# Layer-3 products of a four-layer conditional residual network as fp32 products on halves of the TensorE array

## What is computed

```python
x = x + L0(x)   # x @ W0.T + b0 + scale * (x @ A0[id0].T) @ B0[id0]   rank 16, 8 adapters
x = x + L1(x)   # x @ W1.T + b1 + (x @ A1[id1].T) @ B1[id1].T         rank 16, 32 adapters
x = x + einsum('bsi,boi->bso', x, W2[id2])     # one of 8 matrices 1024 x 1024 for each batch
x = x + einsum('bct,bcd->bdt', x, W3[id3])     # one of 16 matrices 64 x 64, over the 64 tokens
```

## Time and profile before

| | us |
|---|---|
| median of 3 runs | 582.42 (582.11 to 583.15) |
| the profiled execution | 582.33 |
| its span (first to last instruction) | 580.5 |
| PE busy | 571.4 (98% of the span) |
| DVE busy | 326.8 (56%) |
| ACT busy | 282.0 (49%) |
| line 1302, the transposes: 256 matmuls | 35.9 |

### The profile page before, as it was taken

How to read it: one execution, slowest core, us unless ns; L and a number is a source line. 1 busy time by engine, 2 the same in 40 slices (tenths; PEclk the granted TensorE clock), 3 DMA queues, 4 the chain that set the end, 5 groups by cost and what they waited for, 6 DMA issues and landing times.

```text
span 580.5 us, 10596 instructions
## 1 busy us (share of the span) xinstructions
PE 571.4 (98%) x2710; PEld 478.6 (82%) x2711; DVE 326.8 (56%) x583; ACT 282.0 (49%) x370; POOL 56.0 (10%) x87
## 2 busy tenths in 40 slices
PE   8999999999999999999999999999999989999997
PEld 7888888888878888888888888888888878888885
DVE  6985211122777557944455795545588568745320
ACT  5632210214645738646273865536386648455211
POOL 3240000200000300001030000004000202000000
PEclk9999999999999999999999999999999999999999
DMA  8755835101207223453221445322233632230103
GB/s 305 266 176 66 87 99 199 40 20 54 91 25 268 74 56 131 149 183 93 57 63 48 136 124 213 88 60 60 52 126 100 246 87 78 61 101 5 37 2 73
DMA packets 66014, 60.92 MB, mean 105 GB/s; under 512 B 42050, under 2 KB 50242, under 8 KB 65988
## 3 DMA queue, kind: packets, MB, share of 16 engines
q1 hardware_dynamic: 65988, 60.63, 35.4%
HBM read 49.33 MB, written 11.27 MB: 104 GB/s over the span
## 4 chain that ended last, share of the span: by engine, by line
PE 96%; DVE 2%; DMA 1%; ACT 0%; issue 0%; DVEq 0%; POOL 0%; SPq 0%; POOLq 0%
PE y_ps L1271 29%; PE y_ps L1313 27%; PE y_ps L1221 11%; PE t_ps L1221 6%; PE t_ps L1302 5%; PE low_ps L1261 3%; PE y_ps L1341 3%; PE y_ps L1202 2%; PE y_ps L1198 1%; PE low_ps L1202 1%; PE t_ps L1202 1%; PE y_ps L1287 1%; PE y_ps L1286 1%; PE y_ps L1327 1%; PE t_ps L1212 1%; DMA arena<-w 1%
## 5 line engine op out<-in xcount | busy, mean ns | idle before, releaser
L1271 PE MATMUL y_ps<-wm,ops 128*128 128x512 f32 x768 | 179.7, 391 | 0.0
L1271 PEld LDWEIGHTS y_ps<-wm,ops 128*128 128x128 f32 x768 | 141.9, 188 | 29.0 <-DVE arena L1001 0.2
L1313 PE MATMUL y_ps<-ring,ops 128*128 128x512 f32 x696 | 165.3, 390 | 0.0
L1313 PEld LDWEIGHTS y_ps<-ring,ops 128*128 128x128 f32 x696 | 128.9, 188 | 25.5
L581 ACT CAST ops<-arena 128x512 fp32r<-128x512 f32 x32 | 19.7, 620 | 90.6 <-PE y_ps L1271 90.6
L1221 PE MATMUL y_ps<-ring,wm 128*128 128x512 f32 x240 | 55.3, 390 | 0.0
L1221 PEld LDWEIGHTS y_ps<-ring,wm 128*128 128x128 f32 x240 | 44.9, 188 | 9.3
L994 DVE TENSOR_TENSOR ring<-arena,ring 128x1024 fp32r<-128x1024 f32 x40 | 47.7, 1227 | 2.5 <-ACT ring L612 1.7
L483 POOL TENSOR_TENSOR arena<-arena,ident 128x128 f32<-128x128 f32 x40 | 28.3, 727 | 179.4 <-DMA arena<-wt 176.8
L612 ACT CAST ring<-arena 128x1024 fp32r<-128x1024 f32 x40 | 40.5, 1050 | 5.5 <-POOL arena L483 2.3
L1008 DVE TENSOR_TENSOR arena<-arena,ops 128x512 f32<-128x512 f32 x32 | 22.3, 696 | 36.0 <-ACT arena L635 26.3
(11 more groups left out here) (153 smaller groups left out, 635.9 us busy)
## 6 DMA issues: line engine op xcount, KB each, us to landing
arena<-wt SPq DMA_DIRECT2D x48, 512.0 KB, 4.4
arena<-xt SPq DMA_DIRECT2D x32, 256.0 KB, 2.8
out<-arena SPq DMA_DIRECT2D x30, 256.0 KB, 3.1
arena<-w SPq DMA_DIRECT2D x8, 576.0 KB, 5.3
a_stage<-a_tab SPq DMA_DIRECT2D x64, 64.0 KB, 1.9
arena<-b_tab SPq DMA_DIRECT2D x64, 64.0 KB, 2.0
arena<-a_cols SPq DMA_DIRECT2D x8, 256.0 KB, 4.2
a_tab<-bias SPq DMA_DIRECT2D x4, 256.0 KB, 8.4
```

Source lines behind the costliest of these rows:

```text
L1271: op = nc.tensor.matmul(y_ps[:, cols], xs[:, k, part_x, :], wm[:, k, part_w, cols], start=k == 0 and part_x == part_w, stop=False)
L1313: op = nc.tensor.matmul(y[:, cols], xs2[:, k, part_x, :], ring[:, k, part_w, cols], start=k == 0 and part_x == part_w, stop=k == KT - 1 an ...
```

## The change

The transposes become fp32 products without any splitting. For each block of 128 features and each batch there is one product: stationary operand the batch's 64 token rows by 128 features of x2 (rows 0 to 63 or 64 to 127 of the array), moving operand that batch's 64 x 64 matrix. The 16 results of a pair are 64 columns each, the first batch's in one bank of t_ps and the second's in the other, so both banks hold the whole pair, and one block stands where there were two. The splits of x2 and of the matrix go, `xs2_hi` becomes one copy and `xs2_lo` one subtraction for each half, and the second half's copy waits for the first half's subtraction.

Four things come with it. Pair 0's `main_part` and `lora_b` write y2_ps (`main_ps`) and wait for one more product of M. In pair 1 the first half of `main_part` stands ahead of `low_products`, the transposes of pair 0 stand between, and `between_loras` comes two feature blocks later; VectorE's steps 0 and 1 are reordered. SyncE loads the second half of slot 0 (with b0's columns) first, then A1's columns, then the first half; ScalarE and TensorE use the halves as they come. `WARM_UPS` is 9 in place of 11. `layer3_of(j)` waits for `t_done` and is issued a pair later.

```diff
-WARM_UPS = 11
+WARM_UPS = 9
...
+        def main_ps(j):
+            return y2_ps if isinstance(j, int) and j == 0 else y_ps
...
-            load_slot(0)
+            half = HK * P
+            sp.dma_start(slot(0)[:, half:FEATS + N0_COLS], w0[0][:, half:]).then_inc(w0_part_in, 16)
+            sp.dma_start(slot(0)[:, FEATS + N0_COLS:], a1_cols[0]).then_inc(a1_in[0], 16)
+            sp.dma_start(slot(0)[:, 0:half], w0[0][:, 0:half]).then_inc(slot_in[0], 16)
...
             def layer3_of(j):
-                sp.wait_ge(w3_lo_ready, j)
+                sp.wait_ge(t_done, j)
                 load_w3(j)
...
+                if k == 0:
+                    act.wait_ge(w0_part_in, 16)
+                    nc.scalar.copy(w0_blocks(k, 0, second), w0_of[:, second]).then_inc(w0_part_hi, 1)
                 act.wait_ge(a1_in[k % STAGES], 16 * (k // STAGES + 1))
                 nc.scalar.copy(a1[:, k, 0, :], slot(k)[:, FEATS + N0_COLS:]).then_inc(a1_hi, 1)
                 act.wait_ge(w0_folded, k + 1)
-                nc.scalar.copy(w0_blocks(k, 0), ...).then_inc(w0_hi, 1)
+                if k == 0:
+                    nc.scalar.copy(w0_blocks(k, 0, first), w0_of[:, first]).then_inc(w0_hi, 1)
...
             def xs2_hi(j, h, second):
                 def parts(by_batch):
-                    act.wait_ge(t_done, 2 * j + (h + 1))
+                    act.wait_ge(t_done, j + 1)
+                    if h == 1:
+                        act.wait_ge(xs2_lo_ready, 2 * j + 1)
                     if not (isinstance(j, int) and j == 0):
                         act.wait_ge((half_used, l2_done)[h], j)
-                    nc.scalar.copy(xs2_of(h, 0, by_batch), t_of(0)).then_inc(xs2_hi_ready, 1)
-                    nc.scalar.copy(t_lo_of(h), t_of(1)).then_inc(t_lo_ready, 1)
+                    nc.scalar.copy(xs2_of(h, 0, by_batch), t_of(h)).then_inc(xs2_hi_ready, 1)
...
                 dve.wait_ge(y_done, j + 1)
                 if not (isinstance(j, int) and j == 0):
-                    dve.wait_ge(xs2_lo_ready, 2 * j)
-                nc.vector.tensor_tensor(x2, y_ps[:, :], bias[:, :], ALU.add).then_inc(x2_ready, 1)
+                    dve.wait_ge(t_done, j)
+                nc.vector.tensor_tensor(x2, main_ps(j)[:, :], bias[:, :], ALU.add).then_inc(x2_ready, 1)
...
+                    dve.wait_ge(xs2_hi_ready, 2 * j + (h + 1))
+                    nc.vector.tensor_tensor(xs2_of(h, 1, by_batch), t_of(h), xs2_of(h, 0, by_batch),
+                                            ALU.subtract).then_inc(xs2_lo_ready, 1)
...
-                    pe.wait_ge(w0_hi, k + 1)
-                    for i in range(KT):
+                    if k == 0:
+                        pe.wait_ge(w0_part_hi, 1)
+                        pe.wait_ge(a1_hi, 1)
+                    else:
+                        pe.wait_ge(w0_hi, k + 1)
+                    for i in (*SECOND_HALF, *FIRST_HALF):
+                        if k == 0 and i == 0:
+                            pe.wait_ge(w0_hi, 1)
...
-                for k in range(HK):
-                    cols = slice((h * HK + k) * P, (h * HK + k + 1) * P)
-                    to = t_ps[:, 2 * k * P:2 * (k + 1) * P]
-                    for part_x in range(2):
-                        op = nc.tensor.matmul(to, x2_split[:, part_x, cols], w3_split[:, :, :].rearrange("p s r -> p (s r)"),
-                                              start=part_x == 0, stop=part_x == 1)
+                pe.wait_ge(x2_ready, j + 1)
+                pe.wait_ge(w3_folded, j + 1)
+                if not (isinstance(j, int) and j == 0):
+                    pe.wait_ge(xs2_lo_ready, 2 * j)
+                for k in range(KT):
+                    for b in range(2):
+                        r, to = slice(b * ROWS, (b + 1) * ROWS), b * BANK + k * ROWS
+                        op = nc.tensor.matmul(t_ps[:, to:to + ROWS], x2[r, k * P:(k + 1) * P], w3_stage[r, r],
+                                              start=True, stop=True)
...
+            def first_step():
+                low_products(0)
+                pe.wait_ge(m_lo, KT - 1)
+                main_part(0, 0)
+                between_loras(0)
+                pe.wait_ge(m_lo, KT)
+                main_part(0, 1)
+                lora_b(0)
+
+            def second_step():
+                pe.wait_ge(x_lo_ready, 3)
+                main_part(1, 0)
+                low_products(1)
+                transposes(0)
+                main_part(1, 1, {KT - 2: lambda: between_loras(1)})
+                lora_b(1)
+                layer2(0, lambda: transposes(1))
```

More of the change, by code:

```diff
@@ L529, in a_split_of, with w0_blocks @@
             return a_split[:, :, cols].rearrange("p k (b r) -> p b k r", b=2)
-        def w0_blocks(k, part):
-            return wm[:, :, part, k * P:(k + 1) * P]
+        def w0_blocks(k, part, blocks=slice(0, KT)):
+            return wm[:, blocks, part, k * P:(k + 1) * P]
         @block.scalar
@@ L536, in _ @@
             for k in range(KT):
+                w0_of = slot(k)[:, 0:FEATS].rearrange("p (i m) -> p i m", m=P)
+                first, second = slice(0, HK), slice(HK, KT)
+                if k == 0:
+                    act.wait_ge(w0_part_in, 16)
+                    nc.scalar.copy(w0_blocks(k, 0, second), w0_of[:, second]).then_inc(w0_part_hi, 1)
                 act.wait_ge(a1_in[k % STAGES], 16 * (k // STAGES + 1))
@@ L1263, in low_products, with main_part @@
                 op.then_inc(low_done, 1)
-            def main_part(h, between=None):
+            def main_part(j, h, between={}):
                 for k in (FIRST_HALF, SECOND_HALF)[h]:
-                    if between and k == KT - 1:
-                        between()
+                    if k in between:
+                        between[k]()
                     for part_x, part_w in SPLIT:
                         for cols in BANKS:
-                            op = nc.tensor.matmul(y_ps[:, cols], xs[:, k, part_x, :], wm[:, k, part_w, cols],
+                            op = nc.tensor.matmul(main_ps(j)[:, cols], xs[:, k, part_x, :], wm[:, k, part_w, cols],
                                                   start=k == 0 and part_x == part_w, stop=False)
@@ L1361, in layer2 @@
                     batch_half(y_ps, 0, 1, tiles=True)
-                    between(0)
+                    between()
                     pe.wait_ge(xs2_lo_ready, 2 * i + 2)
@@ L1373, in layer2 @@
                         batch_half(y2_ps, 1, 0)
-                        between(1)
                 with pe.Else():
@@ L1388, in layer2, with step @@
                     else:
-                        layer2_half(y, 1, between=lambda: between(1))
-            def step(j, before=1):
-                low_products(j)
-                if not (isinstance(j, int) and j == 0):
-                    pe.wait_ge(x2_ready, j)
-                else:
-                    pe.wait_ge(m_lo, KT - 2)
-                if before >= 2:
-                    pe.wait_ge(first_taken, j - 1)
-                main_part(0)
-                between_loras(j)
-                if before == 0:
-                    pe.wait_ge(m_lo, KT)
-                if before == 1:
-                    transposes(0, 0)
-                main_part(1, (lambda: transposes(0, 1)) if before == 1 else None)
+                        layer2_half(y, 1)
+            def first_step():
[14 more added lines that the diff above has]
+                layer2(0, lambda: transposes(1))
+            def step(j):
+                low_products(j)
+                pe.wait_ge(x2_ready, j)
+                pe.wait_ge(first_taken, j - 1)
+                main_part(j, 0)
+                between_loras(j)
+                main_part(j, 1)
                 lora_b(j)
-                if before >= 1:
-                    layer2(j - 1, lambda h: transposes(j, h))
+                layer2(j - 1, lambda: transposes(j))
             pe.wait_ge(ident_ready, 1)
@@ L1428, in _ @@
             pe.wait_ge(plan_ready, 1)
-            step(0, before=0)
-            step(1)
+            first_step()
+            second_step()
             with pe.Fori(2, PAIRS) as j:
-                step(j, before=2)
-            layer2(PAIRS - 1, lambda h: None, y=y_ps, last=True)
+                step(j)
+            layer2(PAIRS - 1, lambda: None, y=y_ps, last=True)
 def kernel(x, itok_B_1_7, itok_B_6_15, itok_B_3_7, itok_B_0_15, L0_cond_weight, L0_cond_bias,
```

90 lines of the change are left out of this document (23 added, 67 removed).

## The result

| | before | after |
|---|---|---|
| median | 582.41 us (8 runs, 581.95 to 585.28) | 585.18 us (8 runs, 584.25 to 587.69) |
| ratio | | 1.005, 95% interval 1.0032 to 1.0068 |
| profiled execution, span | 582.33, 580.5 | 587.69, 585.7 |
| mean granted clock in the profiled execution | 0.999 | 0.996 |

Slower by 0.5%, which is 2.8 us: a small loss, but clear of zero, where no change was forecast.

What follows compares the result with a forecast made beforehand. The prediction took TensorE to bound the kernel, busy for all 25.75 us of a pair. 582.33 + 2.9 - 2.1 - 1.15 gave 582.0 us, no change, with a range of 574 to 592.

Steps and rivals of the forecast that it cites:

- Terms 1 and 2: Transposes of 16 pairs: old blocks out, 30.7 us; new fp32 products in, 33.6 us; together +2.9 us.
- Rival 1: New transpose blocks: loads of the two halves queue, 3.86 us a block, +31.0 us, 610.1 us; chance 0.16.
- rival 2: New transpose blocks: no price for going in and out, 1.81 us a block, 577.3 us; chance 0.16.
- Rival 3: Start: fewer warm-ups make the clock rise later, start term +0.7 us, 583.8 us; chance 0.04 within the main case.
- its list of what would show it: Signs in the trace: block about 2.1 us, pair about 25.9, no PE wait over 0.3 between 169 and 187, low-part products at 7.8.
- Term 3: Pair 1, up to layer 2: about 2.1 us of TensorE waits all go, -2.1 us.
- The check on what is late next: Pair 1: finish_low(1) would end about 183.4 and TensorE want it at 183.8, fitting by 0.4 us.
- Term 4: Start: with slot 0 loaded in halves, low-part products begin at 7.8 instead of 8.96, -1.15 us.

Runs made afterwards that it cites:

- experiment 3: experiment 1's kernel with all 8 products of the first batch ahead of the 8 of the second, instead of alternating; 613.37 us, one run.
- experiment 4: experiment 1's kernel with both products of a block reading rows 0 to 63, leaving out the second batch's tokens in layer 3; 615.09 us, one run.
- experiment 2: experiment 1's kernel with one fp32 product over all 128 rows per feature block, against the block-diagonal matrix; 579.23 us, ratio to before 0.9953.
- experiment 1: The changed kernel with the load of pair 1's layer-3 matrix ahead of the six layer-2 chunk loads in SyncE's program; 583.99 us, ratio to before 1.0032.
- experiment 5: experiment 2's kernel with finish_low(1) ahead of xs2_lo(0, 0) and x's low part in VectorE's second step; 578.69 us, ratio to before 0.9936.
- experiment 6: experiment 2's kernel with the start of before: whole slot 0 in one load, 11 warm-ups, products in order; 579.89 us.

## Why the prediction was wrong

**What held.** The bound: PE is on the path for 97% in after, and the work taken from the other two engines was worth nothing. The block: 2.12 to 2.14 us measured, 2.10 forecast, from a load of 0.11, pairs of loads side by side, 0.09 going in and 0.09 plus a load coming out. Terms 1 and 2 together are 16 x 0.20 to 0.22, +3.2 to +3.5 where +2.9 stood. Rival 1 (all loads in a row, 610) has its place in experiments 3 and 4, whose programs queue and take 613 and 615, and not in this program; rival 2 (no price for the switch) fell at the first row of the block, and experiment 2 shows what it had asked for: without a change of shape there is none. Rival 3 came true in part: the first products of after did start 0.4 to 0.6 us apart instead of 0.23, but the next ones waited for the copy anyway, so it cost nothing that shows. The clock that did cost time fell at 194.8, where no rival looked.

**The step that failed** is the sentence in the sum that "the moved load of the matrix of layer 3 (issued right behind the transposes, wanted 20 us later)" costs nothing. That is so in the loop. In pair 1 it is neither: the load stands behind `first_chunks(1)` and `b_rows(2)` in SyncE's program, so it was issued 8 us after the transposes of pair 0 and wanted about 4.5 us after that (186.37 to 190.83), with 3 MB in the queue ahead of it. Before, the split had emptied the staging tile at 165.6; now TensorE reads the tile itself, up to 178, and the reload can't come sooner than that. The prediction gave the load's place in the loop and didn't walk the queue for pair 1; its list of what would show it watched PE for waits only up to 187. Price: 1.9 us in the profiled execution, 1.0 to 1.2 in the medians (experiment 1). This step alone doesn't turn the forecast round: experiment 1 has no such wait and is still 1.8 us above before, more than the 1.16 that the prediction counts as no change. The rest is the size of three terms.

**Term 3** was -2.1 and measured -1.55 without the block's own price: from 169.64 to layer 2's first product, which starts in truth at 185.27 because it waits for its load, are 15.63 us against 16.96 before, and one new block in it costs 0.22 more. The check on what is late next looked at the data of `lora_b` (183.4 against 183.8, and it did fit) and not at the 2.1 us that TensorE's own program needs behind that wait; experiment 5 gives 0.54 us of it back.

**Term 4** was -1.15 and measured -0.15 in after's profile, -0.46 to -0.66 in the medians of experiments 2 and 6. The assumption that "the last part lands with the same bytes behind it" was off: cut in three, the slot's last piece released GpSimd between 5.32 and 6.48, against 5.42 and 5.26 with the whole slot.

**The sum again**: +3.2 to +3.5, - 1.55, - 0.15 is +1.5 to +1.8, and experiment 1, which has no wait for the matrix, measured +1.8 over before; with 1.0 to 1.2 for the wait it is +2.5 to +3.0, against +2.8 measured. The clock's 1.6 us are seen in one profiled execution; by their mean clock two of the eight had them, and without these two the median of after is 585.02, 0.16 less. The way from the forecast of -0.4 to +2.8 is made, about, of 1.0 to 1.2 (the wait), 1.0 (the start), 0.55 (layer 2 late) and 0.3 to 0.6 (the block's size).

## What to carry to other kernels

Where an operand is used straight from its staging tile instead of through a split copy, the tile is busy longer, and its next load moves behind whatever stands in the DMA queue: walk the queue in the special first rounds, not only in the loop. Where TensorE has to wait, look also at what its program has to do between that wait and the next long stretch, 2.1 us here. Two products on halves of the rows, side by side, won nothing over one on all rows: both make 16 steps of 0.11 us of a pair's transposes, and the halves pay two changes of shape on top. The plain fp32 product on all rows does them in 1.80 us, against 1.92 split in fp32r and 2.14 on halves, and with the two reorderings of experiments 1 and 5 the kernel is at 578.69 us, 0.64% below the kernel before.

## What the runs showed of the hardware

- Loads for rows 0 to 63 and 64 to 127 run at the same time when they are neighbours in program order (32 records in 16 steps of 0.11 us), hardly when they are 16 records apart (28 steps), and never for the same rows (31 steps). The Trainium skill, TensorEngine Tiling (Array Packing), section Key Properties, says that different tiles can load and multiply in parallel; the trace agrees for neighbours.
- Changing from products of 128 rows to fp32 products of 64 rows and 64 columns, and back, costs 0.09 us on each side and one load of 0.11 that nothing covers; the first load of the block isn't fetched ahead. Changing between fp32r and fp32 at 128 rows costs nothing measurable.
- The clock can fall without TensorE standing still: four times in the one execution with grouped half-row products (3.4 us three times, 6.8 once, at 0.50), twice in the one with single half-row products, each time right at or behind a block of them; not in any of the profiled executions with full rows. In after it fell behind a standstill of 1.9 us and such a block together. Each fall of 3.4 us cost about 1.6 us. It is not only theirs: with the old start and full rows two of eight executions took 582.5 and 582.6 us with a mean clock of 0.997 and 0.996, and no trace shows where.
- The same three loads at the start released GpSimd between 5.3 and 6.5 us in six profiled executions with the same program for the start, which is as much as the whole gain that was forecast from cutting them.
